# Cross-attention with 16 heads of 32: values in four column tiles, softmax sums from pairs added on DVE

## What is computed

```python
x = x + xattn(layernorm(x), ctx, mask, ...)     # x 4 x 512 x 512, ctx 4 x 1601 x 512
x = x + ffn(layernorm(x), ...)                  # 512 -> 2048 -> 512

q, k, v = x @ Wq.T + bq, ctx @ Wk.T + bk, ctx @ Wv.T + bv     # 16 heads of 32
scores = einsum('bhsd,bhtd->bhst', q, k) / sqrt(32)           # 4 x 16 x 512 x 1601
probs  = softmax(clip(where(mask, scores, -10000), -50, 50))
ctx    = einsum('bhst,bhtd->bhsd', probs, v)
delta  = ctx @ Wo.T + bo
```

## Time and profile before

| | |
|---|---|
| three runs, median (range) | 1822.95 us (1821.27 to 1826.97) |
| the profiled execution: its own time | 1820.51 us |
| its span | 1818.6 us |
| mean granted clock of TensorE | 0.951 |

### The profile page before, as it was taken

One profiled execution on the slowest core, in us unless ns is written; L12 is line 12 of the kernel. 1 busy time (PEld: TensorE's weight loads), 2 busy tenths in 40 slices (PEclk: granted clock), 3 DMA queues, 4 the chain that ended last, 5 costly groups with the idle time before them and its releaser, 6 DMA issues. The chain is left out here.

```text
span 1818.6 us, 21753 instructions
## 1 busy us (share of the span) xinstructions
PE 1615.9 (89%) x9048; PEld 1044.3 (57%) x9048; DVE 808.1 (44%) x1217; ACT 727.3 (40%) x885; POOL 179.2 (10%) x95
## 2 busy tenths in 40 slices
PE   4878989999999999999999933765999999999998
PEld 3667433486333873337833312543788888888887
DVE  6512475422555215552255526998333333333433
ACT  2322567633777227773277711233211211121211
POOL 0055630000000000000000014453000000000000
PEclk9989899998999999999999976886999999999999
DMA  6343210120000300002000041574700100110001
GB/s 187 139 150 114 63 30 7 32 77 24 7 7 7 102 24 7 7 7 99 4 7 7 7 146 54 195 273 179 295 29 24 47 23 24 46 46 0 24 23 70
DMA packets 56451, 118.87 MB, mean 65 GB/s; under 512 B 14921, under 2 KB 35785, under 8 KB 50473
## 3 DMA queue, kind: packets, MB, share of 16 engines
q1 hardware_dynamic: 53704, 108.01, 17.2%
q0 software_dynamic: 2656, 9.57, 1.8%
HBM read 78.51 MB, written 39.06 MB: 65 GB/s over the span
## 5 line engine op out<-in xcount | busy, mean ns | idle before, releaser
L505 ACT ACTIVATE cx_probs<-cx_sc,proj_mbias 128x1024 f32<-128x1024 f32 (+1 forms) x416 | 440.5, 1110 | 145.5 <-PE cx_sc L580 145.2
L540 DVE TENSOR_SCALAR cx_probs<-cx_probs 128x1024 f32<-128x1024 f32 (+1 forms) x416 | 306.5, 746 | 257.0 <-ACT cx_probs L505 257.0
L594 PE MATMUL cx_acc<-cx_probs,cx_vt 128*64 128x512 f32 (+1 forms) x1664 | 407.4, 611 | 11.0 <-DVE cx_probs L540 11.0
L594 PEld LDWEIGHTS cx_acc<-cx_probs,cx_vt 128*64 128x64 f32 (+1 forms) x1664 | 102.0, 137 | 210.2 <-issue 143.3
L580 PE MATMUL cx_sc<-cx_q,cx_kt 32*128 32x512 f32 (+1 forms) x2496 | 203.8, 428 | 9.7 <-ACT cx_probs L505 6.8
L580 PEld LDWEIGHTS cx_sc<-cx_q,cx_kt 32*128 32x128 f32 (+1 forms) x2496 | 102.4, 182 | 188.5 <-ACT cx_probs L505 167.9
L126 PE MATMUL cx_sc<-proj_cs,proj_wk 128*128 128x256 f32 (+1 forms) x1344 | 176.0, 290 | 34.5 <-DVE cx_kt L525 23.3
L126 PEld LDWEIGHTS cx_sc<-proj_cs,proj_wk 128*128 128x128 f32 x1344 | 170.9, 198 | 43.2 <-DVE cx_kt L525 27.2
L1081 ACT ACTIVATE ff_silu<-ff_gp,ff_scale 128x512 f32<-128x512 f32 x64 | 44.1, 689 | 368.0 <-PE ff_gp L126 368.0
L126 PE MATMUL ff_yp<-ff_wds,ff_hs 128*128 128x512 f32 x768 | 189.6, 396 | 0.2 <-DVE ff_hs L1119 0.2
L1116 DVE SCALAR_TENSOR_TENSOR ff_hf<-ff_up,ff_scale,ff_silu 128x512 f32<-128x512 f32 x64 | 48.1, 751 | 288.9 <-ACT ff_silu L1081 288.9
(11 more groups left out here) (131 smaller groups left out, 1474.2 us busy)
## 6 DMA issues: line engine op xcount, KB each, us to landing
proj_raw<-in_ctxT SPq DMA_DIRECT2D x24, 512.0 KB, 5.1
scr_q<-qu_qs SPq DMA_DIRECT2D x4, 2048.0 KB, 6.3
cx_q<-scr_q SPq DMA_DIRECT2D x4, 2048.0 KB, 8.0
scr_wd<-pr_wds SPq DMA_DIRECT2D x4, 2048.0 KB, 12.8
ff_wds<-scr_wd SPq DMA_DIRECT2D x8, 1024.0 KB, 4.7
scr_xs<-hand_xs SPq DMA_DIRECT2D x3, 2048.0 KB, 7.9
ff_xs<-scr_xs SPq DMA_DIRECT2D x3, 2048.0 KB, 18.6
qu_xt<-in_x SPq DMA_DIRECT2D x4, 1024.0 KB, 10.4
```

Of the source, the lines that this page charges most:

```text
L505: nc.scalar.activation(probs[N % NB][0:r], sc[N % NSC][0:r], ACT.Exp, bias=mbias[0:r, b, t:t + 1], scale=SCALE).then_inc(exp_done, 1)
L540: nc.vector.tensor_scalar(probs[N % NB][0:r], probs[N % NB][0:r], LOW, HIGH, ALU.max, ALU.min).then_inc(clip_done, 1)
L594: last = nc.tensor.matmul(acc[z][half * 2 * HD:(half + 1) * 2 * HD], own, probs[N % NB][0:r, half], start=t == 0, stop=t == TT - 1)
```

## The change

- The ones leave `vt`. `values` has four matmuls of 32 columns in a step, one for each head, in four column tiles, all into one bank `acc`, and waits for both clips of the step. It runs a step later than the first half did before.
- The sums have a bank of their own, `tot`. DVE adds the buffers of two neighbouring tiles (`add`): for pair j of a group, the first buffers (z = 0) in step t = 2j+1 and the second (z = 1) in step t = 2j+2, each 128 x 1024 into `padd`. PE multiplies them with a constant 128 x 32 of ones in two halves of 256 columns (`sums`), in the steps t = 3 to 11; the last three halves of a group are owed until t = 0 to 2 of the next (`owed`). The 13th tile has no partner and is summed alone (`single`).
- An exp waits for the values and the addition that read its buffer (or the single sum). There are six buffers.
- DVE copies `acc` after a clip of t = 1, and `tot` after a clip of t = 2. SP stores two transfers for each group, not eight.
- The first two context pieces of the next batch are split at the end of the projections, before the exps.
- POOL does the butterflies in eight parts of half the width, two under the projections of each batch; its first instruction sets 128 x 32 ones.

```diff
@@ -386,9 +386,11 @@
 
     STEPS = HC * TT
     PAIRS_B = 2 * STEPS
-    NSC, NB = 3, 5
+    NSC, NB = 3, 6
+    QP = TT // 2
+    SUMS = 2 * QP + 1
     SCALE = 1.0 / float(np.sqrt(HD))
-    FLY = 4
+    FLY = 8
     IC = INTER // P
     FW = H // FLY
     STAGES = IC.bit_length() - 1
@@ -396,22 +398,31 @@
...
-        vt = m.sb("vt", [P, TT, NH // 2, 3, HD])
+        vt = m.sb("vt", [P, TT, H])
+        ones = m.sb("ones", [P, HD])
         q = m.sb("q", [P, 2, HC, S], F32R)
         probs = [m.sb(f"probs{i}", [P, 2, S]) for i in range(NB)]
-        ob = [m.sb(f"ob{z}", [P, S]) for z in range(2)]
+        padd = [[m.sb(f"padd{z}_{i}", [P, 2, S]) for i in range(2)] for z in range(2)]
+        ob, os = m.sb("ob", [P, S]), m.sb("os", [P, S])
         fl = [m.sb(f"fl{i}", [P, IC, FW]) for i in range(2)]
         sc = [m.ps(f"sc{i}", [P, 2, S]) for i in range(NSC)]
-        acc = [m.ps(f"acc{z}", [P, S]) for z in range(2)]
+        acc, tot = m.ps("acc", [P, S]), m.ps("tot", [P, S])
 
...
-        STORES = 8
+        STORES = 2
+
+        def sums_until(g, j):
+
+            return g * SUMS + 2 * j + 2 + (1 if j >= QP - 2 else 0)
+
+        SINGLE = 2 * QP - 2
 
...
@@ -429,14 +440,10 @@
 
                 def store(b, c):
                     g = b * HC + c
-                    for z in range(2):
-                        sp.wait_ge(acc_out[z], g + 1)
-                    for r in range(HC):
-                        z, half = r % 2, r // 2
-                        ctx = half * 2 * HD + z * HD
-                        tot = half * 2 * HD + (1 - z) * HD
-                        sp.dma_start(scr["c"][b, r * HD:(r + 1) * HD, c], ob[z][ctx:ctx + HD]).then_inc(stored, 16)
-                        sp.dma_start(scr["sum"][b, 4 * c + r], ob[z][tot:tot + 1]).then_inc(stored, 16)
+                    sp.wait_ge(acc_out, g + 1)
+                    sp.dma_start(scr["c"][b, :, c], ob[:]).then_inc(stored, 16)
+                    sp.wait_ge(tot_out, g + 1)
+                    sp.dma_start(scr["sum"][b, 4 * c:4 * c + 4], os[0:P:HD]).then_inc(stored, 16)
 
...
@@ -451,9 +458,9 @@
 
             @block.gpsimd
             def _(pool):
-                nc.gpsimd.memset(vt[:, :, :, 1], 1.0).then_inc(pads, 1)
-
-                for part in range(FLY):
+                nc.gpsimd.memset(ones[:], 1.0).then_inc(pads, 1)
+
+                def butterflies(part):
                     cols = slice(part * FW, (part + 1) * FW)
                     base = part * 2 * STAGES
                     if part:
@@ -471,12 +478,18 @@
                         nc.gpsimd.tensor_tensor(di[:, :, 1], si[:, :, 0], si[:, :, 1], ALU.subtract).then_inc(fly, 1)
                     pool.wait_ge(fly, base + 2 * STAGES)
                     pool.dma_start(scr["wdb"][:, :, cols], fl[STAGES % 2][:]).then_inc(fly_out, 16)
+
+                for b in range(B):
+                    at_least(pool, exp_done, b * PAIRS_B)
+                    for part in range(b * FLY // B, (b + 1) * FLY // B):
+                        butterflies(part)
                 pool.wait_ge(fly_out, FLY * 16)
 
             @block.scalar
             def _(act):
                 def context_hi(b, p):
-                    at_least(act, v_done, (b * TT + FROM[p - 2] + PIECE) if p >= 2 else b * TT)
+                    old = NP + p - 2
+                    at_least(act, v_done, (b - 1) * TT + old // NP * TT + min(FROM[old % NP] + PIECE, TT))
                     proj.split_hi(nc, act, b, p)
...
@@ -492,8 +505,7 @@
                     for t in range(FROM[p], min(FROM[p] + PIECE, TT)):
                         n = rows_of(t)
                         act.wait_ge(v_done, b * TT + t + 1)
-                        nc.scalar.activation(vt[0:n, t, :, 0:3:2], sc[1][0:n, t % 2].rearrange("p (g z d) -> p g z d", z=2, d=HD),
-                                             ACT.Copy).then_inc(v_out, 1)
+                        nc.scalar.activation(vt[0:n, t], sc[1][0:n, t % 2], ACT.Copy).then_inc(v_out, 1)
 
                 def exps(b):
                     for n in range(PAIRS_B):
@@ -501,17 +513,25 @@
                         c, t = divmod(n // 2, TT)
                         r = rows_of(t)
                         act.wait_ge(scores_done, N + 1)
-                        at_least(act, values_done, N - NB + 1)
+                        old = (N - NB) // 2
+                        if old >= 0:
+                            act.wait_ge(values_done, old + 1)
+                            og, ot = divmod(old, TT)
+                            if ot < TT - 1:
+                                act.wait_ge(added[n % 2], og * QP + ot // 2 + 1)
+                            else:
+                                act.wait_ge(sums_done, og * SUMS + SINGLE)
                         nc.scalar.activation(probs[N % NB][0:r], sc[N % NSC][0:r], ACT.Exp, bias=mbias[0:r, b, t:t + 1],
                                              scale=SCALE).then_inc(exp_done, 1)
-                        if b + 1 < B and n == PAIRS_B // 2:
-                            context_hi(b + 1, 0)
-                            context_hi(b + 1, 1)
 
                 for b in range(B):
                     for p in range(NP):
                         keys_hi(b, p)
+                        if p == NP - 1 and b + 1 < B:
+                            context_hi(b + 1, 0)
                         values_out(b, p)
+                    if b + 1 < B:
+                        context_hi(b + 1, 1)
                     exps(b)
 
             @block.vector
...
-                def collect(b, c, z):
+                def collect_values(b, c):
                     g = b * HC + c
-                    dve.wait_ge(values_done, b * PAIRS_B + 2 * TT * (c + 1) - 1 + z)
+                    dve.wait_ge(values_done, (g + 1) * TT)
                     at_least(dve, stored, g * STORES * 16)
-                    nc.vector.tensor_copy(ob[z][:], acc[z][:]).then_inc(acc_out[z], 1)
+                    nc.vector.tensor_copy(ob[:], acc[:]).then_inc(acc_out, 1)
+
+                def collect_sums(b, c):
+                    g = b * HC + c
+                    dve.wait_ge(sums_done, (g + 1) * SUMS)
+                    at_least(dve, stored, g * STORES * 16)
+                    nc.vector.tensor_copy(os[:], tot[:]).then_inc(tot_out, 1)
+
+                def add(b, c, j, z):
+                    g = b * HC + c
+                    i = b * STEPS + c * TT + 2 * j
+                    dve.wait_ge(clip_done, 2 * i + 3 + z)
+                    if j >= 2 or g:
+                        dve.wait_ge(sums_done, sums_until(g, j - 2) if j >= 2 else sums_until(g - 1, QP + j - 2))
+                    nc.vector.tensor_tensor(padd[z][(g * QP + j) % 2][:], probs[(2 * i + z) % NB][:], probs[(2 * i + 2 + z) % NB][:],
+                                            ALU.add).then_inc(added[z], 1)
 
                 def clips(b):
                     for n in range(PAIRS_B):
@@ -538,18 +573,23 @@
                         r = rows_of(t)
                         dve.wait_ge(exp_done, N + 1)
                         nc.vector.tensor_scalar(probs[N % NB][0:r], probs[N % NB][0:r], LOW, HIGH, ALU.max, ALU.min).then_inc(clip_done, 1)
-                        if t == 0 and c and n % 2 == 0:
-                            collect(b, c - 1, 1)
-                        if t == TT - 1 and n % 2 == 1:
-                            collect(b, c, 0)
-                        if b + 1 < B and n == PAIRS_B // 2:
-                            proj.split_lo(nc, dve, b + 1, 0)
-                            proj.split_lo(nc, dve, b + 1, 1)
-                    collect(b, HC - 1, 1)
+                        if c and n % 2 == 0 and t == 1:
+                            collect_values(b, c - 1)
+                        if c and n % 2 == 1 and t == 2:
+                            collect_sums(b, c - 1)
+                        if t % 2 and n % 2:
+                            add(b, c, t // 2, 0)
+                        if t and t % 2 == 0 and n % 2:
+                            add(b, c, t // 2 - 1, 1)
+                    collect_values(b, HC - 1)
+                    collect_sums(b, HC - 1)
 
                 for b in range(B):
                     for p in range(NP):
                         keys_lo(b, p)
+                    if b + 1 < B:
+                        proj.split_lo(nc, dve, b + 1, 0)
+                        proj.split_lo(nc, dve, b + 1, 1)
                     clips(b)
 
             @block.tensor
@@ -574,26 +614,57 @@
...
-                        for h in (0, 2, 1, 3):
-                            N = b * PAIRS_B + 2 * i + h % 2
+                        for h in range(HC):
+                            N = b * PAIRS_B + 2 * i + h // 2
                             own = slice(h * HD, (h + 1) * HD)
-                            last = nc.tensor.matmul(sc[N % NSC][0:r, h // 2], kt[own, z, c, t * P:t * P + r], q[own, y, c],
+                            last = nc.tensor.matmul(sc[N % NSC][0:r, h % 2], kt[own, z, c, t * P:t * P + r], q[own, y, c],
```

(56 more changed lines are left out.)

7 lines of the change are left out of this document (4 added, 3 removed).

## The result

The changed kernel takes 1840.37 us (median of four runs, 1837.51 to 1845.35) against 1823.62 for the kernel before: ratio 1.0093, 95% interval 1.0066 to 1.0121. It is slower, by 17 us. The profiled execution took 1837.51 with a span of 1835.7, 17.1 longer than the span before.

The account below looks back on a forecast made before the run. PE was taken to bound the kernel before, the ring of six buffers the changed steps. +21.0 − 20.4 − 2.8 − 2.6 + 1.0 + 1.0 + 12.0 = +9.2 on 1820.5 gave 1829.7, median 2.4 above: 1832, range 1803 to 1856.

Parts of the forecast that it names:

- PE in a step: PE's work in one attention step: 2.34 us instead of 2.77, about 2.37 on average with the single sum.
- Rival 1: Attention matmuls: column tiles do not pack, a step takes 4.3 us, +320 us (+190 if only neighbours pair); chance 0.05.
- The ring: Six probability buffers: exps of odd steps wait for DVE's additions, 5.41 us for two steps, 2.70 a step.
- Rival 2: Attention steps: the ring does not bind, steps of 2.37 us, 1785 or 1773 us in all; chance 0.06.
- The border: Groups 2 and 3 of a batch: the sums' copy at t = 2 stalls, 37.4 us against 36.0, PE idle 3.3.
- The undisturbed batch: First exp of a batch to the first of its last step: 143.4 us against 139.8, +3.6.
- What goes: Savings: excess of the first three batches −20.4 us, POOL's memset −2.8, last stores −2.6.
- The memset's 2.8: Ahead of the first projection: POOL's memset sets 32 columns instead of 3328, −2.8 us.
- The clock: Behind the 12 group borders: 10 followed by a half-clock stretch at 1.2 us each, +12 us.
- rival 4: Group borders: the clock falls oftener or costs 2 us each, 24 to 26 us instead of 12, 1845; chance 0.15.
- Between the batches: Behind a batch's last exp: single sum and three halves +1.9 us a batch; POOL beside the projections +1.
- The ends: Kernel start: memset −2.8 us, split before batch 0's exps +1.0; kernel end: sums behind last exp +1.9, stores −2.6.

Follow-up runs that it names:

- seven buffers: The changed kernel with seven probability buffers instead of six, DVE's order kept: 1783.82 us, ratio 0.9773 to the kernel before.
- The moves without the tiles: The kernel before with POOL's rotations in eight parts under all projections and the next batch's first splits ahead of the exps: 1805.83 us, ratio 0.9900.
- the two kernels with the moves alone: The kernel before with only POOL's rotations moved under the projections, 1812.86 us; the same with the splits moved ahead of the exps too, 1805.83 us.
- seven buffers, three pairs: The changed kernel with seven buffers, the sums' copy in t = 3, three pairs of sum buffers and POOL's work in 32 parts: 1735.08 us, ratio 0.9506.

## Why the prediction was right, step by step

The time came out at 1840.4 for a forecast of 1832 and a range of 1803 to 1856; slower was the likeliest of the three. The mechanism in the batches is the one forecast, and its numbers hold closely; the clock's term and both ends were off, in part against each other.

- **PE in a step.** 2.34 forecast, 2.33 found. Values 0.88 for 0.91; the sums' half with its switch 0.55 for 0.52. Rival 1 (the tiles do not pack) is refuted: four column tiles run side by side, two rounds for four f32 matmuls. The eight instructions of the values at 205.35 start in two bunches of four, 0.007 us apart within a bunch and 0.45 from one bunch to the next. The rule of "TensorE: Matmul & The Clock Gate", Part 3, "The mechanism", in the Trainium skill (starts and ends in strict program order) therefore doesn't add rounds here; it was my inference from it, that a tile's second instruction holds back the other tiles, that was wrong.
- **The ring.** Forecast 5.41 for two steps, 2.17 and 3.24; found 5.43, 2.17 and 3.26. The wake of 0.11, the middle of a guess, is 0.11. Rival 2 is refuted, and seven buffers show that it was the ring and not DVE's load.
- **The border.** Forecast 5.8, found 5.88; PE idle 3.3, found 3.32; a group 37.4, found 37.5 where the clock held.
- **The undisturbed batch.** Forecast 143.4; found 33.7 + 37.5 + 37.5 + 35.4 = 144.1 from the quietest groups. Against 139.8 that is +17.3 in four batches, for +14.4 forecast. The 33.7, of batch 2, is not free of the half clock (granted 0.95), so a part of this +2.9 is the clock's.
- **What goes.** All 20.6 us of excess were counted but 0.2. The moves without the tiles gave 17.2 in the batches; the rest came back as small drops of the clock. The memset's 2.8 is there: the first projection starts at 103.19 and not at 106.21.
- **The clock: this is the term that was mis-sized.** I took 10 of 12 borders at 1.2 us, +12. Found are 8 of 12, with 1.2 to 3.0 us each, 14.8 together, and 2.9 more in the first groups of batches 0, 1 and 3 (34.7 instead of 33.7), where PE also stands still at the start: +17.7. Fewer borders than I counted, and dearer each; it was part of rival 4. That the two errors partly cancel is luck. The start of a batch I had not looked at, though the kernel before shows it too (steps of 2.85 to 3.49 in batch 0). Nor did PE stand still in one place only, as I wrote: the splits made it pause for 1.45 to 1.46 us in the middle of batches 0, 1 and 2, and only batch 1's pause was followed by the half clock. By that count a border was less sure to draw it than my 10 of 12.
- **Between the batches.** Tail, splits and POOL were put at 5.7 + 1.0 = 6.7 for three; +6.0 found.
- **The ends.** The first exp of batch 0 comes 5.9 us sooner, where memset and split make 1.8: the projections of batch 0 also ran at a higher clock. POOL's and the splits' moves are not the cause: in the two kernels with the moves alone the first of the windows below has 0.80, and the first exp comes later than before. What raised it was not traced. Windows of the kernel before:

```profile
106.00:120.00 14.00, 13.79 (x79) 12.83 (x80) 1.94 (x4) 3.04 (x6) 4.99 (x4) 0.85 0.79 272
...
165.00:180.00 15.00, 14.96 (x87) 13.70 (x88) 2.68 (x6) 3.80 (x8) 8.84 (x5) 0.89 0.46 131
```

and of the changed kernel, 0.99 for 0.85 and 1.00 for 0.89:

```profile
106.00:120.00 14.00, 14.00 (x96) 13.04 (x96) 2.42 (x5) 4.63 (x9) 6.02 (x5) 0.99 0.67 223
...
165.00:180.00 15.00, 15.00 (x91) 13.30 (x90) 2.31 (x5) 4.17 (x9) 0.00 (x0) 1.00 0.12 35
```

The last stretch is 2.5 longer instead of 0.7 shorter. The load of the sums comes 0.2 sooner after the exps, and 2.7 are lost behind it, in parts which the change doesn't touch: PE is busy there for 651.1 us instead of 649.1, with as many instructions. Why was not traced.

Against the forecast, term by term, that is +5.7 for the clock, +2.9 for the batches, −0.2 for the excess, −0.7 between, −4.1 at the start and +3.2 at the end: +6.8, and 1.0 from a slip of mine (3.6 + 1.9 a batch was carried as 5.3, and not as 5.5). The two ends nearly cancel, which is luck, and the forecast had neither.

## What to carry to other kernels

An engine's busy share says what it could save, not what a step will cost: after a change of the loads, write down for each buffer which instruction frees it and in which step that one is issued, and add the loop up. Two such loops were in this kernel, one for the probabilities and one for their sums, and with the copy moved, loosening the first alone gave 1785 us, for the second then held the time; loosening both gave 1744. A copy with a wait belongs where its data is ready, behind the work of its engine that others wait for: the same copy one step later was worth 41 us of 1840.

## What the runs showed of the hardware

A stall costs more than its length: where PE had 0.12 of 3.40 us of work, the next windows had a granted clock of 0.66 and 0.84. That came behind 8 of 12 pauses of 3.32 us, and such a group took 1.2 to 3.0 us longer. Repeating scores whose result is thrown away, in order to keep PE busy, was 14 us cheaper than standing still (1826 for 1840). And the stretch from PE's last matmul of a batch to the first scores of the next took 90.0, 89.0 and 84.7 us within one execution (seven buffers), at a granted clock of 0.92, 0.94 and 0.98, so a part that a change doesn't touch can move by several microseconds. DVE was slower beside POOL: an addition of 1.22 us took 1.48, a clip of 0.69 mostly 0.95 (seven buffers, three pairs).
